# A windowed attention and convolution kernel: the loop over its four images written out

## The reference

```python
x0 = gn(x)                                  # mean and variance per image and channel
xw = windows(x0)                            # 64 windows of 16x16 per image
q, k, v = (ln(shuffle_invert(conv3(xw, w, b), 2)) for w, b in (q, k, v))   # 64 tokens x 128
attn = softmax(q @ k.T * SCALE + bias)      # 8 heads of 16
out = pixel_shuffle((attn @ v) @ proj_w.T + proj_b, 2)
xr = image(xw + out)
y = xr + conv3(gelu(conv3(xr, c1w, c1b)), c2w, c2b)
return x + y
```

## Time and profile before

| what | value |
|---|---|
| median of 3 runs | 852.89 us (851.65 to 853.03) |
| the profiled execution | 853.24 us |
| its span, first to last instruction | 851.1 us |
| PE busy | 761.1 us, 89% |
| DVE busy | 660.4 us, 78% |
| ACT busy | 605.7 us, 71% |
| POOL busy | 483.2 us, 57% |
| images begin (first product, L993) | 32.11, 231.14, 435.78, 639.91 us |
| the outer loop's branch on PE | 247.6, 452.0, 656.6 us |

### The profile page before, as it was taken

How to read it: one execution, slowest core, us unless ns; L and a number is a source line. 1 busy time by engine, 2 the same in 40 slices (tenths; PEclk the granted TensorE clock), 3 DMA queues, 4 the chain that set the end, 5 groups by cost and what they waited for, 6 DMA issues and landing times.

```text
span 851.1 us, 19126 instructions
## 1 busy us (share of the span) xinstructions
PE 761.1 (89%) x5704; PEld 537.6 (63%) x5704; DVE 660.4 (78%) x2142; ACT 605.7 (71%) x1287; POOL 483.2 (57%) x1041
## 2 busy tenths in 40 slices
PE   0479999999788999999888999999989899999988
PEld 0347777766356777767445777776735677777753
DVE  6558888878657888878675888887866788888575
ACT  1498888765478888876457888877556888886651
POOL 5468677752237777764144776776233677776410
PEclk9999999999999999999999999999999999999999
DMA  7110123000231030300052013110014212000004
GB/s 250 56 29 30 48 108 106 1 1 1 87 125 55 28 128 0 106 1 2 1 166 70 29 30 126 52 55 1 1 56 137 64 34 78 0 1 2 1 1 148
DMA packets 17655, 47.14 MB, mean 55 GB/s; under 512 B 2080, under 2 KB 2720, under 8 KB 17568
## 3 DMA queue, kind: packets, MB, share of 16 engines
q1 hardware_dynamic: 17568, 46.09, 16.6%
HBM read 37.69 MB, written 8.39 MB: 54 GB/s over the span
## 4 chain that ended last, share of the span: by engine, by line
PE 44%; issue 19%; DVE 16%; POOL 11%; ACT 8%; DVEq 1%; DMA 0%; SPq 0%; ACTq 0%; POOLq 0%
PE y_ps L998 12%; PE o_ps L1065 7%; PE pt_ps L1055 5%; PE s_ps L1044 5%; POOL ln_rs L715 4%; PE s_ps L1087 4%; DVE ln_st L540 3%; ACT qk_n L840 3%; PE ox_ps L1014 3%; PE y_ps L969 2%; ACT sc L855 2%; PE t_ps L1023 2%; ACT v_bd L848 2%; DVE h_hi L509 2%; PE y_ps L993 1%
## 5 line engine op out<-in xcount | busy, mean ns | idle before, releaser
L840 ACT ACTIVATE qk_n<-y_ps,ln_nr,ln_rs 128x128 f32<-128x128 f32 x256 | 103.5, 456 | 81.8 <-POOL ln_nr L718 81.1
L998 PE MATMUL y_ps<-w_hi,x_hi 128*128 128x192 f16 (+1 forms) x512 | 149.9, 293 | 0.0
L998 PE MATMUL y_ps<-w_hi,x_lo 128*128 128x192 f16 (+1 forms) x512 | 149.5, 292 | 0.0
L998 PE MATMUL y_ps<-w_lo,x_hi 128*128 128x192 f16 (+1 forms) x512 | 149.5, 292 | 0.0
L728 POOL TENSOR_TENSOR sc<-sc,mx 128x512 f32<-128x512 f32 x128 | 133.7, 1045 | 22.0 <-DVE mx L566 21.5
L1065 PE MATMUL o_ps<-v_bd,pt 128*128 128x66 f32 x1024 | 128.6, 268 | 0.0
L1065 PEld LDWEIGHTS o_ps<-v_bd,pt 128*128 128x128 f32 x1024 | 124.5, 192 | 0.2
L551 DVE TENSOR_TENSOR sc<-s_ps,biasS 128x512 f32<-128x512 f32 x128 | 86.5, 676 | 47.4 <-PE s_ps L1044 45.4
L540 DVE BATCH_NORM_STATS2 ln_st<-y_ps 128x6 f32<-128x128 f32 x384 | 88.7, 286 | 42.6 <-PE y_ps L998 35.5
L715 POOL TENSOR_TENSOR ln_rs<-ln_ve,neg_half 128x3 f32<-128x3 f32 x128 | 113.0, 883 | 10.7
L711 POOL TENSOR_TENSOR ln_ve<-ln_mv,eps_y 128x3 f32<-128x3 f32 x128 | 24.8, 194 | 154.1 <-DVE ln_mv L545 153.8
(11 more groups left out here) (161 smaller groups left out, 1636.5 us busy)
## 6 DMA issues: line engine op xcount, KB each, us to landing
xs<-in_x_sh_dram SPq DMA_DIRECT2D x32, 576.0 KB, 3.9
xst<-in_x_al_dram SPq DMA_DIRECT2D x16, 512.0 KB, 6.8
xf<-in_x_al_dram SPq DMA_DIRECT2D x32, 256.0 KB, 4.2
out_dram<-xf SPq DMA_DIRECT2D x32, 256.0 KB, 2.4
wst<-in_wqkv_dram SPq DMA_DIRECT2D x1, 768.0 KB, 3.8
w1s<-in_w_dram SPq DMA_DIRECT2D x1, 256.0 KB, 8.7
w2s<-in_w_dram SPq DMA_DIRECT2D x1, 256.0 KB, 8.7
biasS<-in_bias_t_dram SPq DMA_DIRECT2D x1, 256.0 KB, 9.4
```

Of the source, the lines that this page charges most:

```text
L840: ins = act.activation(qk_n[j][:, t, :].rearrange("p (h y x) -> p h y x", h=HEADS, y=2), by_head(y_ps[j][:, E * t:E * (t + 1)]), ACT.Identity,
L998: ins = pe.matmul(y.rearrange("p (t e) -> p t e", t=3)[:, :, cols], xx[r % 2][:, s, a % 2, 2 * TS * (a // 2):2 * TS * (a // 2 + TS)], ww[: ...
```

## The change

`images` is a Python loop now, which writes the code of an image four times into each engine's program, with b a number instead of a register. The inner loop over the steps stays a hardware loop and now stands in four places instead of two. In every place outside it the counts and addresses are constants. No computation is added, removed or moved. The calls lose their first argument:

```diff
--- before.py
+++ after.py
@@ -280,11 +280,10 @@
         BORDER1 = 10
 
 
-        def images(e, image):
-
-            with e.Fori(0, B - 1) as b:
-                image(b, True)
-            image(B - 1, False)
+        def images(image):
+
+            for b in range(B):
+                image(b, b < B - 1)
 
         def has(n):
             return 0 <= n < PAIRS
@@ -347,7 +346,7 @@
                 load(dst, src, loaded_consts)
             for r in range(2, 4):
                 row(0, r)
-            images(sp, image)
+            images(image)
             for i in range(NXF):
                 sp.wait_ge(stored[i], 16 * B * T2N // NXF + 16)
 
@@ -644,7 +643,7 @@
             start_scales(0)
             head(0, step)
             low_conv_weights()
-            images(v, image)
+            images(image)
 
         @block.gpsimd
         def _(pool):
@@ -743,7 +742,7 @@
 
             begin(0, True)
             head(0, step)
-            images(pool, image)
+            images(image)
 
         @block.scalar
         def _(act):
@@ -924,7 +923,7 @@
 
             act.wait_ge(gn_chain, 7)
             head(0, step, lambda b, t: start_xr(t - 5) if t >= 5 else None)
-            images(act, image)
+            images(image)
 
         @block.tensor
         def _(pe):
@@ -1119,7 +1118,7 @@
             head(0, step)
 
             pe.wait_ge(c_scales, 1)
-            images(pe, image)
+            images(image)
 
 
 def _phases(n):
```

## The result

| | before | after |
|---|---|---|
| median | 852.70 us (851.65 to 853.03, 4 runs) | 846.48 us (845.47 to 847.05, 4 runs) |
| ratio | | 0.9928 [0.9911, 0.9945] |
| profiled execution, its span | 853.24, 851.1 us | 846.25, 844.4 us |

The written-out loop is 6.2 us faster by the medians and 6.7 us by the two spans. The forecast was a gain of 5.5 us, 847.4 us, with a range of 845.2 to 850.2. The time lies in the range, 0.9 us under the forecast.

What follows compares the result with a forecast made beforehand. The prediction took PE to lead (busy 89%), with DVE's stall at the image loop's branch on the chain. It summed 4.65 + 0.72 + 0.1 = 5.47, rounded to 5.5 us, off 852.89: 847.4 us, range 845.2 to 850.2.

Steps and rivals of the forecast that it cites:

- What bounds the kernel at the border: Between images, DVE's 2.59 and 2.34 us idle before its first statistics lie on the chain; PE's and ACT's stalls run beside.
- The cause, a fetch of the loop's start: At the image loop's taken branch, the start is no longer held near the engine and must be fetched: 3940 against 78 ns.
- Rival (d): At each image's start, the stall is first code after a long wait and stays: 852.9 us, no change; chance 0.03.
- The price of the two back edges, 4.65 us: Ways into images 1 and 2 exceed the exit's into image 3 by 2.60 + 2.05 us; bounds 4.1 and 4.93 us.
- Rival (c): Part of the gain is given back to PE's clock or late fetches: gain 1.7 to 4, 850.0 us; chance 0.06.
- Rival (b): Stretches between images also lose register work and a low-clock stretch: gain 6.3 to 8, 845.8 us; chance 0.10.
- Register arithmetic, 0.72 + 0.1 = 0.82 us: Computed wait numbers become constants: 0.24 us in steps 20 to 26 of three images, 0.1 for first steps and heads.
- Rival (a): Only the image loop's branches count, DVE's register work is covered: gain 4.1 to 4.9 us, 848.4 us; chance 0.15.
- SP at nothing: Register instructions ahead of SP's transfers go; reloads starting 0.1 or 0.2 us earlier are covered by ACT's 0.94 us wait: 0.
- Longer code at nothing: The written-out program costs 0, since straight code is fetched ahead in time, as in image 3's first-run middle.
- rival (e): The inner loop's back edges, now in four places, begin to miss: slower, 855.6 to 857.8 us; chance 0.04.
- The changed profile's signs: At image starts, no issue idle on DVE or PE; ways in about 58.3 us, pair 18 to 18 about 201.8 us.

Runs made afterwards that it cites:

- e5_act: The changed kernel with the image loop kept on ACT only, written out on the other engines: 847.33 us, ratio 0.9925 to the kernel before.
- The hint: The kernel before, image loop kept on every engine, with a prefetch hint for its closing branch at the start of each pass: 850.17 us, ratio 0.9954.
- e4_pe: The changed kernel with the image loop kept on PE only, written out on the other engines: 846.95 us, ratio 0.9923 to the kernel before.
- e2_regs: The changed kernel, but images 0 to 2 take their image number from a register, so register arithmetic stays: 846.87 us, ratio 0.9920 to the kernel before.
- The filled pair: The kernels before and after, each with throwaway products on PE where it waits between images: 851.90 us (0.9981) and 844.70 us (0.9894).
- e12_before_fill: The kernel before, loop kept, with throwaway products on PE where it waits between images: 851.90 us, ratio 0.9981 to the kernel before.
- e3_dve: The changed kernel with the image loop kept on DVE only, written out on the other engines: 853.27 us, ratio 0.9994 to the kernel before.

## Why the prediction was right, point by point

**What bounds the kernel at the border: right for DVE.** DVE's stall ahead of L540 is the one on the path. Looping on DVE alone costs all of the gain (0.9994), and a prefetch on DVE alone gives it back (0.9915). PE's and ACT's stalls were read as shorter and beside it. By the time they cost nothing, 0.9923 and 0.9925 with the loop on one of them. At an equal clock PE's back edge costs 0.8 to 1.3 us once DVE no longer stalls. What it costs beside DVE's stall, no run shows. That ACT's 1.92 us was the same kind of stall, although the row named PE, is shown by e5_act.

**The cause, a fetch of the loop's start: right.** The hint leaves branch and arithmetic in place and takes 2.59 us to 0.22, and a 16 KB packet of instructions comes within each of PE's slow branches in e4_pe. Rival (d), first code after a wait, is out, since no image of after has a stall.

**The price of the two back edges, 4.65 us: right as a net sum, wrong as the price of the stalls.** The step was to take the exit as the same work without a branch. It was the same work, but at a granted clock of 0.94; two stretches of 1.2 GHz lie in it, one at its start (3.41 us from 639.64) and one in the first steps (from 666.95). The prediction saw the clock and concluded the wrong thing from it: that the exit won in spite of it. It should have taken the low clock out of the reference. With kernels that have no stall and one stretch at the same place as before had it, e2_regs, the two stalls are 60.96 - 57.77 = 3.19 and 60.40 - 58.09 = 2.31, together 5.5 us. The filled pair gives 60.38 - 57.70 = 2.68 for image 1, with one stretch of 3.41 us on both sides, and e12_before_fill by itself gives 2.49 + 2.53 = 5.0 us. So a stall costs 2.3 to 3.2 us, and the two together 5.0 to 5.5 us. That is more than DVE's idle times, which the prediction had called the upper bound: 4.93 us in before, and 4.72 in e12_before_fill.

**What the clock took back.** In after, each way in has the last 5.3 of 6.83 us at 1.2 GHz and takes 58.3 to 58.4 us where 56.7 is possible: 1.7 us. In before the taken ways in had 1.1 to 1.4 of it (the 57.77 and 58.09 us of e2_regs, less 56.70). The change gave back 0.3 to 0.6 us in each of two images, and nothing in the third. Net: 5.5 - 0.9 = 4.6 us, the measured saving of the ways in; this is the same rows taken apart over e2_regs and not a check of its own. The forecast hit it because its reference, the exit, carried 1.66 us of low clock and every way in of after carries 1.6 to 1.7. The prediction gave no reason for that agreement, so it is luck. Rival (c) was right in kind (given back to the clock) and not in size. Rival (b), a gain of 6.3 us and up, is not far off either, with 6.2 us by the medians and 6.7 by the spans: the stretches between images did shorten by register work (1.0 us), and the low clock in the first steps (from 260.76, 465.56 and 666.95 us before) is gone in after. But one of twice the length stands in each head in its place.

**Register arithmetic, 0.72 + 0.1 = 0.82 us: the term that was mis-sized; it is 2.0 us.** Middles gave 1.06 and tails 0.96 us. Two steps failed. The 0.24 us came from steps 20 to 26 alone, and there it is right, 0.26 us. But the whole middle of image 3 in before was already 0.26 to 0.31 us shorter than the others (81.28 against 81.54 to 81.59), and 81.21 in after. And "for the last steps, the c1 and c2 tiles and the heads ... I count nothing": the argument was that the difference from image 2 to image 3 stays as it was up to pair 31. It does, but it ends there; image 3 has no following image, so before holds no tail without registers, and the tail was worth 0.32 us an image. The bound of 0.8 us was stated for image 0's first steps and the heads; for the tails there was none. e2_regs shows both parts at once, 81.52 and 62.13 us with no branch anywhere. Rival (a), branches alone, is out. That the arithmetic runs "mostly while the operation before it still runs" fits DVE, whose loop adds nothing from pair 18 to pair 26; ACT's adds 0.15 us there, and POOL's or SP's 0.09.

**SP at nothing: holds.** With POOL and SP looping, the ways into images 1 and 2 (57.90 and 57.82 us, one stretch of 3.41 us each) are like those of e2_regs at the same clock, and the tail (61.85) is that of after. The 0.1 us of its middle may be POOL's or SP's; no run tells these two apart.

**Longer code at nothing: right.** The program is longer, yet the instruction queues move less: 42 and 45 packets on the page of before, 37 and 38 on that of after. No new idle time put down to issue stands at the images' starts. With the inner loop written out as well, the middle gets shorter, not longer. Where prediction and the Trainium skill ("Runtime: NRT & Kernel Launch", section "Instruction fetch mechanics") met, the skill's rule is that a taken branch stalls when it leaves the window of two pages. For the outer loop the trace agrees, with 2.59 us on DVE and up to 4.1 us on PE. For PE's inner loop it does not. The prediction counted the kernel's calls, 226 products and near 500 instructions. The trace has more: 292 products, 292 weight loads and 46 others, 630 between the two branches of a pass. That is more than two pages of 256, and still the branch takes 243 ns at most, at four places in the program. So rival (e) is out by measurement.

**The changed profile's signs.** L539 right behind L607, no idle time on PE, inner branches only and under 0.3 us: all as written. The ways in were to be about 58.3 us and are 58.31 to 58.41. From pair 18 to the next pair 18 it was to be 201.8 us and is 201.44, 201.44 and 201.37: shorter by 0.32 us of tail. This was the one sign in the profile that spoke of the mis-sized term. The signs did not name the longer wait of PE in the heads and its low clock there.

## What to carry to other kernels

When a profile has the same work twice, once with the cost in question and once without, the difference is the best price there is; but lay the granted clock beside it, and look for the part of the work that the second copy doesn't have. A hardware loop with a long body stalled PE, DVE and ACT at each back edge here, and the stall that set the time was DVE's, which reaches its branch with nothing queued to cover the wait: ask for a prefetch there, or write the loop out. Compare two kernels' pieces at an equal clock before calling a cost nothing; PE's loop seemed free by the time and was not. Once a stall is gone, look at what the next engine does with the time; here TensorE waited longer between images and fell to 1.2 GHz, and a few products that nobody reads were worth another 0.2 to 0.3%.

## What the runs showed of the hardware

- The hint makes the slow branch quick on PE and DVE: PE's row from 3940 to 462 ns at median, DVE's idle time from 2.59 to 0.22 us. DVE's branch row itself gets longer by it, 75 against 63 ns at median, and an image's middle by 0.12 us.
- PE's queue runs ahead of its products. Its branch row of 3.32 us left 0.39 us of idle time (e4_pe, first back edge), since some 3.2 us of products were already on their way; the second, of 4.10 us, left 1.60. DVE's branch is reached only as its last operation starts, and 2.59 us of its stall are seen.
- POOL and SP, whose bodies are short, branch back in 40 to 55 ns with no stall. Counted in the profile's rows, the image loop's body has 92 instructions on SP, 277 on POOL, 400 on ACT, 609 on DVE and 2421 on PE; the last three stall. Where between 277 and 400 the border lies, or whether it is the same for all engines, no run shows. PE's inner loop of 630 doesn't stall.
- The clock at an image's first product goes with how long PE has waited there for DVE's yt. In the ten kernels without filling products, images 1 to 3, PE waited 3.8 to 4.1 us in 7 cases of 30, and was granted 1.2 GHz during the wait or within 0.7 us behind it in all 7; it waited 2.2 to 2.7 us in the other 23, and the clock fell there in 5. In the three kernels with filling products it waited 0.8 to 1.1 us, and the clock fell in none of 9. So the length of the wait doesn't decide alone, and what in PE's activity does stays open.
- A stretch of low clock can keep another away. The longer wait of after comes from an earlier PE: in before, 3.41 us at 1.2 GHz (from 216.39 us) slow the tiles ahead of this place, which costs nothing by itself (the tail is 61.84 us in e3_dve with such a stretch and 61.83 in after without), and make PE's wait 2.46 us and not 3.83. In the same 30 cases the wait is 3.8 us or more in all 7 that have no such stretch ahead, and 2.7 us or less in all 23 that have one.
- Register arithmetic for wait counts isn't free: 0.65 us per image here, somewhat over half of it with ACT's loop.
